# A convolution and mixture-of-experts kernel: its chunk loop written out, the gates' exponentials issued earlier, and the gates spread one step sooner into other banks

## The reference, cut to what matters

```python
x = x + conv(sign(_ln_c(x)), ...)       # 3x3 binary conv, batch norm over all images, clipped to [-1, 1]
t = _to_tokens(x)                       # (32, 3136, 64)
def ffn(x):                             # x = _ln_t(t)
    w = softmax(mean(x, axis=0) @ Wr + br)          # one set of 8 gates per position
    h = relu(_bn(einsum('bfd,edh->bfeh', x, W1) + b1))
    h = relu(_bn(einsum('bfeh,ehk->bfek', h, W2) + b2))
    y = einsum('bfeh,ehd->bfed', h, Wo) + bo
    return einsum('bfed,fe->bfd', y, w)
t = t + ffn(_ln_t(t))
```

## Time and profile before

| | |
|---|---|
| time, median of 3 runs (lowest, highest) | 1506.76 us (1502.95, 1511.66) |
| the profiled execution: its time, its span | 1507.65 us, 1505.7 us |
| PE busy | 1374.3 us (91%) |
| DVE busy | 977.6 us (65%) |
| ACT busy | 883.1 us (59%) |
| POOL busy | 544.5 us (36%) |
| mean granted clock of PE | 0.965 |

### The profile page before, as it was taken

One profiled execution on the slowest core, in us unless ns is written; L12 is line 12 of the kernel. 1 busy time (PEld: TensorE's weight loads), 2 busy tenths in 40 slices (PEclk: granted clock), 3 DMA queues, 4 the chain that ended last, 5 costly groups with the idle time before them and its releaser, 6 DMA issues. The chain is left out here.

```text
span 1505.7 us, 36699 instructions
## 1 busy us (share of the span) xinstructions
PE 1374.3 (91%) x12984; PEld 669.0 (44%) x12984; DVE 977.6 (65%) x1660; ACT 883.1 (59%) x1279; POOL 544.5 (36%) x474
## 2 busy tenths in 40 slices
PE   3999965999898999989899898999989899899998
PEld 2666632444344444444444443444444444344444
DVE  5888852667565675656666565776656667566665
ACT  3666654566565665656566565665655566566553
POOL 7000053344244444334344234434334344244441
PEclk9999976999999999999999999999999999999999
DMA  9999722233322233322232322232322233323221
GB/s 156 167 156 149 107 49 49 46 75 66 72 48 53 63 75 63 75 44 63 57 75 66 72 53 52 60 75 63 75 45 63 57 75 66 72 48 64 53 51 32
DMA packets 361591, 107.20 MB, mean 71 GB/s; under 512 B 353552, under 2 KB 353776, under 8 KB 361456
## 3 DMA queue, kind: packets, MB, share of 16 engines
q1 hardware_dynamic: 360192, 103.49, 36.7%
q0 software_dynamic: 1264, 1.61, 0.7%
HBM read 78.97 MB, written 26.09 MB: 70 GB/s over the span
## 5 line engine op out<-in xcount | busy, mean ns | idle before, releaser
L943 DVE SCALAR_TENSOR_TENSOR v<-ps,negb,wb 128x448 f32<-128x448 f32 x896 | 570.0, 677 | 323.6 <-PE ps L580 316.0
L752 ACT ACTIVATE h<-ps,bias 128x896 f32<-128x896 f32 x448 | 451.4, 1007 | 402.1 <-PE ps L555 395.5
L555 PE MATMUL ps<-xc,w 64*64 64x448 f32 x3584 | 456.4, 550 | 47.4 <-issue 36.0
L580 PE MATMUL ps<-h,w 64*64 64x448 f32 x3584 | 459.5, 549 | 0.4 <-ACT vareps L775 0.4
L596 PE MATMUL ps<-v,wo 64*64 64x448 f32 x3584 | 454.6, 547 | 2.0 <-issue 1.5
L555 PEld LDWEIGHTS ps<-xc,w 64*64 64x64 f32 x3584 | 161.7, 134 | 236.8 <-issue 226.0
L462 POOL TENSOR_TENSOR o<-xin,gconst 128x448 f32<-128x448 f32 x112 | 125.5, 1142 | 342.7 <-ACT gconst L793 247.3
L580 PEld LDWEIGHTS ps<-h,w 64*64 64x64 f32 x3584 | 176.9, 135 | 157.2 <-issue 130.9
L596 PEld LDWEIGHTS ps<-v,wo 64*64 64x64 f32 x3584 | 164.5, 135 | 168.8 <-issue 149.5
L470 POOL TENSOR_TENSOR o<-o,upper 128x448 f32<-128x448 f32 x112 | 127.6, 1139 | 264.6 <-DVE o L953 264.6
L440 POOL TENSOR_TENSOR xc<-xc,spread 128x896 f32<-128x896 f32 x56 | 118.2, 2128 | 176.2 <-DMA spread<-rs_rows 176.2
(11 more groups left out here) (151 smaller groups left out, 841.7 us busy)
## 6 DMA issues: line engine op xcount, KB each, us to landing
xa<-in_x SPq DMA_DIRECT2D x64, 392.0 KB, 7.2
xin<-in_x SPq DMA_DIRECT2D x112, 224.0 KB, 4.0
spread<-rs_rows SPq DMA_DIRECT2D x112, 224.0 KB, 4.3
out<-o SPq DMA_DIRECT2D x224, 112.0 KB, 2.5
rs_rows<-rs SPq DMA_DIRECT2D x112, 3.5 KB
rows<-in_L_ffn_g POOLq DMA_DIRECT2D x2, 256.0 KB, 5.8
rows<-in_L_ffn_v POOLq DMA_DIRECT2D x2, 256.0 KB, 6.6
cwt<-in_L_conv_weight SPq DMA_DIRECT2D x2, 144.0 KB, 2.7
```

Of the source, the lines that this page charges most:

```text
L555: last = mm(ps[64 * two:64 * two + 64, L1_BANKS + ab, 0:NG], w1[half, P * q + C * two:P * q + C * two + C], xc[half, s, g // 2, ab ^ (g % ...
L580: last = mm(ps[64 * i:64 * i + 64, L2_BANKS[ab] + low, 0:NG], w2[rows_, Q + QUADS * i, :], h[rows_, u % 2, i, ab, :], start=True, stop=True)
L752: A(h[:, u % 2, i], ps[:, L1_BANKS:L1_BANKS + 2, 0:NG], ACT.Relu, bias=bias[:, 0, q:q + 1]).then_inc(h_done[i], 1)
L943: last = V.scalar_tensor_tensor(out=v[:, u % 2, ab, d, :].rearrange("p (b w) -> p b w", w=W), in0=ps[:, L2_BANKS[ab] + d, 0:NG].rearrange( ...
```

## The change

- `body_of_chunks` has no loop: all 28 chunks are written out on every engine, with constants in place of registers.
- `prep_point` calls chunk k + 1 in front of chunk k + 2, and ACT's `prep` has the exponential at its head. At point 28 ACT thus issues the exponential, then the two centred copies.
- `wb` is at 63 instead of 64: the last point of the chunk ahead, in unit 7. It writes banks 2 and 3 (gates in `Y + 1`, constants in `Y`), which the turn has just used, instead of 4 and 5. `layer2` of unit 0 now waits for `g_done` in its first half, not its second. Chunk 0 has it at point 5 of `AHEAD`.

```diff
             t=(8, 10, 12, 14), x1=(13, 16, 17, 21), centre=(20, 28),
-            var=34, root=36, square=38, inv=(40, 41), logits=58, gate=60, turn=62, wb=64)
+            var=34, root=36, square=38, inv=(40, 41), logits=58, gate=60, turn=62, wb=63)
...
-        def body_of_chunks(chunk, eng):
-
-            chunk(0, 0, True, 2)
-            with eng.Fori(0, RP // 2 - 2) as j:
-                chunk(2 * j + 1, 1, False, 2)
-                chunk(2 * j + 2, 0, False, 2)
-            chunk(RP - 3, 1, False, 2)
-            chunk(RP - 2, 0, False, 1)
-            chunk(RP - 1, 1, False, 0)
+        def body_of_chunks(chunk):
+
+            for k in range(RP):
+                chunk(k, k % 2, k == 0, min(RP - 1 - k, 2))
...
+            if left:
+                prep(STEADY, k + 1, 1 - s, half + HALVES)
             if left > 1:
                 prep(STEADY, k + 2, s, half)
-            if left:
-                prep(STEADY, k + 1, 1 - s, half + HALVES)
-            prep(STEADY, k, s, half + 2 * HALVES)
...
                     if ab == 0 and u == 0:
-                        pe.wait_ge(placed_done, k + 1)
-                        pe.wait_ge(wT_done, k + 1)
+                        pe.wait_ge(g_done, k + 1)
...
-                    if ab == 1 and u == 0:
-                        pe.wait_ge(g_done, k + 1)
...
                     if h == at.wb:
                         pe.wait_ge(placed_done, q + 1)
                         pe.wait_ge(wT_done, q + 1)
-                        pe.wait_ge(v_done[1], UNITS * q + 1)
-                        if isinstance(q, int) and q == 0:
-                            pe.wait_ge(xc_done, 2 * STEPS)
                         pe.sem_inc(wb_free, 1)
                         for hi in range(2):
-                            last = mm(ps[64 * hi:64 * hi + 64, Z, 0:NG], to_half[:, hi, :], placed[:].rearrange("p a w -> p (a w)"),
+                            last = mm(ps[64 * hi:64 * hi + 64, Y + 1, 0:NG], to_half[:, hi, :], placed[:].rearrange("p a w -> p (a w)"),
                                       start=True, stop=True)
...
                 def prep(at, q, s, h):
                     Y, Z = L2_BANKS
+                    if h == at.gate:
+                        act.wait_ge(gate_sub, q + 1)
+                        A(gate_e[:], gate[:], ACT.Exp).then_inc(gate_exp, 1)
```

More of the change, by code:

```diff
@@ L218, in metaformer_kernel @@
             t=(8, 10, 12, 14), x1=(13, 16, 17, 21), centre=(20, 28),
-            var=34, root=36, square=38, inv=(40, 41), logits=58, gate=60, turn=62, wb=64)
+            var=34, root=36, square=38, inv=(40, 41), logits=58, gate=60, turn=62, wb=63)
         AHEAD = Schedule(
             t=(0, 0, 0, 0), x1=(0, 0, 0, 0), centre=(1, 2),
-            var=3, root=3, square=3, inv=(3, 3), logits=5, gate=5, turn=5, wb=64)
+            var=3, root=3, square=3, inv=(3, 3), logits=5, gate=5, turn=5, wb=5)
         def places_at(when, h):
             return [g for g in range(len(when)) if when[g] == h]
-        def body_of_chunks(chunk, eng):
-            chunk(0, 0, True, 2)
-            with eng.Fori(0, RP // 2 - 2) as j:
-                chunk(2 * j + 1, 1, False, 2)
-                chunk(2 * j + 2, 0, False, 2)
-            chunk(RP - 3, 1, False, 2)
-            chunk(RP - 2, 0, False, 1)
-            chunk(RP - 1, 1, False, 0)
+        def body_of_chunks(chunk):
+            for k in range(RP):
+                chunk(k, k % 2, k == 0, min(RP - 1 - k, 2))
         def prep_point(prep, k, s, left, half):
+            if left:
+                prep(STEADY, k + 1, 1 - s, half + HALVES)
             if left > 1:
                 prep(STEADY, k + 2, s, half)
-            if left:
-                prep(STEADY, k + 1, 1 - s, half + HALVES)
-            prep(STEADY, k, s, half + 2 * HALVES)
         def prep_ahead(prep):
@@ L336, in _ @@
                 spread_rs(0, 0)
-                body_of_chunks(chunk, sp)
+                body_of_chunks(chunk)
                 for s in stored:
@@ L490, in _ @@
                 feature(0, 0)
-                body_of_chunks(chunk, pool)
+                body_of_chunks(chunk)
             @block.tensor
@@ L653, in prep @@
                         for par in range(2):
-                            last = mm(ps[64 * par:64 * par + 64, Z + 1, 0:W], expert_const[:, 64 * par:64 * par + 64], wT[:], start=True, stop=True)
+                            last = mm(ps[64 * par:64 * par + 64, Y, 0:W], expert_const[:, 64 * par:64 * par + 64], wT[:], start=True, stop=True)
                         last.then_inc(g_full, 1)
@@ L691, in _ @@
                 prep(AHEAD, 0, 0, AHEAD.logits)
-                body_of_chunks(chunk, pe)
+                body_of_chunks(chunk)
             @block.scalar
@@ L781, in prep @@
                         A(sq[:], rs[:], ACT.Square).then_inc(root_done, 1)
-                    if h == at.gate:
-                        act.wait_ge(gate_sub, q + 1)
-                        A(gate_e[:], gate[:], ACT.Exp).then_inc(gate_exp, 1)
                     if h == at.turn:
@@ L790, in prep @@
                         act.wait_ge(wb_full, q + 1)
-                        A(wb[:, s].rearrange("p a b w -> p (a b w)"), ps[:, Z, 0:NG], ACT.Copy).then_inc(wb_done, 1)
+                        A(wb[:, s].rearrange("p a b w -> p (a b w)"), ps[:, Y + 1, 0:NG], ACT.Copy).then_inc(wb_done, 1)
                         act.wait_ge(g_full, q + 1)
-                        A(gconst[:, s, :], ps[:, Z + 1, 0:W], ACT.Copy, bias=-1.0).then_inc(g_done, 1)
+                        A(gconst[:, s, :], ps[:, Y, 0:W], ACT.Copy, bias=-1.0).then_inc(g_done, 1)
                 def chunk(k, s, first, left):
@@ L816, in _ @@
                 prep(AHEAD, 0, 0, AHEAD.logits)
-                body_of_chunks(chunk, act)
+                body_of_chunks(chunk)
             @block.vector
@@ L1019, in _ @@
                 prep(AHEAD, 0, 0, AHEAD.logits)
-                body_of_chunks(chunk, dve)
+                body_of_chunks(chunk)
 _INS = ["x", "L0_conv_weight", "L0_conv_gamma", "L0_conv_beta", "L0_ffn_Wr", "L0_ffn_br", "L0_ffn_W1", "L0_ffn_b1",
```

## The result

The changed kernel takes 1452.84 us (median of four runs, 1451.34 to 1454.09) against 1506.28 for the kernel before beside it; the ratio is 0.964, 95% interval 0.961 to 0.967. It is faster, but by 53 us where 79 were predicted: 1452.84 lies above the range's high end of 1444.

The account below looks back on a forecast made before the run. PE, busy 91%, was taken to bound the kernel. From 1507.65 profiled, minus 56.5 (loop) and 24.7 (gates), plus 1.3 (supply) and 1.4 (chunk 0), gave 1429.2; less 0.9 for the median, 1428 us, range 1411 to 1444.

Parts of the forecast that it names:

- the charge for instruction supply: In the newly written-out chunks on PE: one more stop inside a matmul group, 1.3 us lost, bounds 0 and 10.4.
- The loop written out: At PE's chunk ends: removing 11 back-branches of 5.1 us each wins 56.5 us, less 1.3 for instruction supply.
- The other terms: The sum without the supply charge: 56.5 us and 24.7 won, 1.4 lost at chunk 0, median 0.9 below the profile.
- The loop's price: At PE's back-branches: idle time and the slow clock behind it cost 5.1 us a branch, 56.5 in all.
- The gates: At chunk ends, exponential ahead of the copies and earlier spread together win 0.95 us at each of 26 ends, 24.7.
- The 1.4 charged ahead of chunk 0: Ahead of chunk 0 the spread waits with no `layer1` group before it: 1.4 us lost, once.
- Only the loop pays: Rival at chunk ends: the new waits for `wT` and `gconst` equal the two removed, 1453 us; chance 0.06.
- Straight code starves PE: Rival in PE's written-out code: each new instruction block stops PE, 84 x 1.32 = 111 us, giving 1538; chance 0.03.
- The low clock comes back: Rival at chunk ends: the new waits bring PE's half clock back, 13 x 1.5 = 20 us, giving 1448; chance 0.03.
- the list of what would show the prediction wrong: In the changed profile: matmul-group stops every 12 us or so, half-clock stretches at chunk ends, or a turn that still waits.

Follow-up runs that it names:

- drift48: The changed kernel with one increment of an unused semaphore behind every group of matmuls on PE (48 a chunk): 1424.90 us, ratio 0.947.
- shift128: The changed kernel with 128 increments of an unused semaphore once on PE, ahead of the chunks, none in them: 1456.18 us, ratio 0.967.
- aligned: The changed kernel with 114 unused semaphore increments spread over each chunk on PE and 191 ahead of all: 1435.47 us, ratio 0.952.
- one8_l3: The changed kernel with one semaphore increment in each unit (8 a chunk), behind the first `layer3` group: 1430.01 us, ratio 0.950.
- one48_before: The kernel before, loop and gates untouched, with one semaphore increment behind every group of matmuls: 1534.33 us, ratio 1.019.
- one42_before: The kernel before with a semaphore increment behind every group of units 0 to 6, none in unit 7: 1524.99 us, ratio 1.013.

## Why the prediction was wrong, and where it was right

**The step that failed** is the charge for instruction supply in "The loop written out": "I charge one more such stop, 1.3; bounds are 0 and one for every three of the 24 chunks that are newly written out, 8 x 1.3 = 10.4". The term measures 28 (1452.84 against 1424.90 with one increment behind each group; 26 by the ratios), over 20 times the charge and 2.7 times its upper bound. Of the 24.7 that the 24 chunks of the two traces give back, 20.2 stand at passages; the rest isn't traced to them. The other terms make 1427.0 without it; with 28 they would have given 1455. I had the evidence in hand, the stop of rows 7, and weighed it by the wrong sample: "Within a round PE runs 85 us of straight code at 42.6 a chunk, so fetching ahead keeps up" was true of the loop, but a loop passes its blocks at the same few places in each round, and these happened to be cheap. The traces bear that out: in the kernel before, the nine packets of a round start at the same records of the round in all ten full rounds, within 35 of some 1,870; increments win next to nothing in the chunks between branches (42.2 to 42.9) and 28 in the written-out code; and with the gates' edits these chunks run at 41.3 to 41.6, without stops. Written out, the same passages drift through the chunk (3.55 blocks each) and meet the dear places. The written-out chunks at the end of the old kernel were the fitting sample, and the upper bound was made from them, one stop of 1.32 in three chunks. Even that was too low by more than half, because only a stop that the idle column names was counted. The reading of rows 9 was wrong too: the packets do shrink without the loop, from 122 to 101, about two for each of the 11 branches taken. It changed nothing in the sum, since the 84 packets charged in the rival are the 85 passages found.

**What a passage costs.** In the changed kernel the 85 passages of 24 chunks cost 22.4 us, some 0.3 each, 0 at many and over 1 at some. The Trainium skill (Runtime: NRT & Kernel Launch, instruction fetch mechanics) has it that crossing to the next block of sequential code is mostly hidden. This trace doesn't agree, and the measurement decides; in `drift48`, with an increment behind each group, 2.2 us are left of the 22.4, as the page has it.

**The loop's price** was right in what it is: no distance of 46 to 49, no 2.9 idle, and the clock stays full. Its size can't be read alone: a branch costs 5.1 with the old gates and 6.35 with the new ones.

**The gates** were right in mechanism and, within what the runs can tell, in size: 25.2 (22 by the ratios) against 24.7, DVE's wait for the exponential 0.37 against 0.4, the spread 1.33 behind the turn against 1.45, and 41.57 from turn to turn in a chunk without stops against the 41.6 to 41.8 forecast. The 1.4 charged ahead of chunk 0 isn't seen: from the first turn to the second it is 43.20, and 44.12 before.

**The rivals.** "Only the loop pays" gave 1453, the time that was measured, and yet is refuted: the gates pay in full, and the supply takes as much. "Straight code starves PE" was the right mechanism with the wrong price, 1.32 for each of 84 packets where some 0.3 is measured; it needed a chance of its own at small prices, not only at the one that turns the sign. "The low clock comes back" didn't happen. And the list of what would show the prediction wrong had it: "stops within a group of matmuls every 12 us or so (the fetch)".

**What stays open** is why one instruction between two groups cures the passages. Without increments the silence of PE's semaphore instructions in which a packet starts is up to 3.8 long (`shift128` 3.5); with them up to 1.9 in `drift48` and 1.4 in `aligned`. That would fit a stream that runs through a block's rest in a burst and comes to the next block before it has landed, some 2.4 to 2.8 after the packet's start, while an instruction at each group keeps it at PE's own pace. But it isn't shown: increments shorten the silences by being stamped themselves, and `one8_l3`, which has most of the gain, still has a silence of 3.2. Nothing here shows where in the stream the next block is asked for. And why satisfied waits cost 0.9 a chunk is open too.

## What to carry to other kernels

Count the instructions of the bounding engine before writing a loop out: here a back-branch was a large visible cost (5.1 us), the passages of straight code were small (0.3) and hidden in the busy share, and both were supply of instructions. If matmul groups in straight code stop with "issue" and no semaphore in their middle, try one idle semaphore increment behind a group or a unit (28 and 21 to 23 us of 1453 here), not many in a row (246 lost), and not in a loop without looking at the branch (29 lost). When a trace holds even one sample of a new regime, price the regime by it, and let the upper bound be one stop for each place where it can happen.

## What the runs showed that I had not expected

- 48 additional instructions a chunk made straight code 1.9% faster (1452.84 to 1424.90, 1.8% by the ratios); 114 in lumps made it 17% slower (1698.47).
- A back-branch's cost isn't a constant: 2.87 of idle in the kernel before, 5.77 in `one48_before`, and 3.24 and 1.09 in two pieces in `one42_before`, and each time PE starts again 2.4 to 3.0 after a packet's start.
- VectorE's sum of 0.61 us takes up to 2.5 when GpSimd's two-input product has begun before it, and begun one or two half-steps sooner, ahead of the product, it takes 0.61. The fourth sum of a chunk meets another product of GpSimd's and still takes up to 2.3 in most chunks.
